# Taking the combination stage out of a graph, mixture-of-experts and LSTM kernel: expert blocks write the final rows

## The reference, cut to what matters

```
x1 = x + L0_gnn(norm(x))                      # first gather over the edges
h  = norm(x1)
idx = argmax(softmax(h @ gate_w)); pos = rank of the token within its expert
kept = pos < 977                               # tokens beyond the capacity get y = 0
y  = expert[idx](h) * (prob * kept)            # two matrix products with a relu between
x2 = x1 + nan_to_num(y)
h2 = norm(x2) @ W
out = segment_sum(dinv[src] * dinv[dst] * h2[src], dst)   # edges, and a self loop for each node
x3 = x2 + leaky_relu(out + b)
```

## Time and profile before

| what | us |
|---|---|
| median of 3 runs (4526.97 to 4539.17) | 4530.03 |
| span of the profiled execution, first to last instruction | 4155.8 |
| experts, 1838 to 2306 | 468 |
| combination, 2306 to 2396 | 90 |
| second gather stage, 2396 to 3426 | 1030 |

### The profile page before, as it was taken

How to read it: one execution, slowest core, us unless ns; L and a number is a source line. 1 busy time by engine, 2 the same in 40 slices (tenths; PEclk the granted TensorE clock), 3 DMA queues, 4 the chain that set the end, 5 groups by cost and what they waited for, 6 DMA issues and landing times. The chain is left out here.

```text
span 4155.8 us, 60925 instructions
## 1 busy us (share of the span) xinstructions
PE 3533.2 (85%) x19537; PEld 2737.7 (66%) x19537; DVE 1869.1 (45%) x5749; ACT 900.6 (22%) x2377; POOL 1671.7 (40%) x1752
## 2 busy tenths in 40 slices
PE   7999999878888888879999455667777779999996
PEld 3444444477777787856666245555555559999996
DVE  4555400133454555643333722233344554444787
ACT  2333333100000011112222500000000004444553
POOL 1000000277777777730110577777777750000000
PEclk9999999887878888869999577787889999999998
DMA  4343444433444444441221643444455555434333
GB/s 149 151 153 150 148 169 168 143 111 113 119 121 131 132 136 139 142 121 43 84 85 54 195 133 106 119 133 133 141 153 159 165 163 163 148 114 121 108 108 114
DMA packets 224399, 544.30 MB, mean 131 GB/s; under 512 B 44131, under 2 KB 125286, under 8 KB 210255
## 3 DMA queue, kind: packets, MB, share of 16 engines
q1 hardware_dynamic: 139744, 314.86, 22.4%
q0 software_dynamic: 80576, 220.31, 18.8%
q10 hardware_dynamic: 3760, 5.24, 0.4%
HBM read 363.08 MB, written 176.74 MB: 130 GB/s over the span
## 5 line engine op out<-in xcount | busy, mean ns | idle before, releaser
L1677 POOL DMA_INDIRECT b_msg<-scratch_gtab,k_src_row x782 | 767.3, 981 | 253.5 <-issue 248.3
L914 POOL DMA_INDIRECT a_msg<-scratch_hrel,k_rel_row x782 | 762.3, 975 | 241.1 <-issue 236.2
L1726 PE MATMUL b_ps<-b_hit,b_msg 128*128 128x128 f32 x3128 | 493.1, 323 | 278.0 <-DMA b_msg<-scratch_gtab,k_src_row 266.4
L706 PE MATMUL r_psm<-k_w,r_xnT 128*128 128x512 f32 x1568 | 693.1, 597 | 5.1 <-ACT r_hst L670 4.2
L1726 PEld LDWEIGHTS b_ps<-b_hit,b_msg 128*128 128x128 f32 x3128 | 460.7, 233 | 350.4 <-issue 270.7
L980 PE MATMUL a_ps<-a_hit,a_msg 128*128 128x128 f32 x3128 | 520.1, 335 | 115.5 <-DMA a_msg<-scratch_hrel,k_rel_row 112.6
L980 PEld LDWEIGHTS a_ps<-a_hit,a_msg 128*128 128x128 f32 x3128 | 479.8, 242 | 146.2 <-DVE a_hit L1102 69.1
L2105 PE MATMUL l_psg<-k_hall,k_whhT 128*128 128x125 f32 x4640 | 550.7, 277 | 5.2 <-DVE k_hall L2231 5.2
L2105 PEld LDWEIGHTS l_psg<-k_hall,k_whhT 128*128 128x128 f32 x4640 | 538.4, 193 | 5.7 <-DVE k_hall L2231 5.7
L706 PEld LDWEIGHTS r_psm<-k_w,r_xnT 128*128 128x128 f32 x1568 | 293.1, 191 | 348.5 <-issue 340.4
L670 ACT COPY r_hst<-r_psm 128x512 f32<-128x512 f32 x392 | 229.2, 586 | 471.6 <-PE r_psm L706 471.6
(11 more groups left out here) (273 smaller groups left out, 3622.4 us busy)
## 6 DMA issues: line engine op xcount, KB each, us to landing
scratch_hrel<-r_hst SPq DMA_DIRECT2D x98, 1024.0 KB
l_xr<-scratch_xrow SPq DMA_DIRECT2D x146, 512.0 KB, 3.6
scratch_xrow<-n_xs SPq DMA_DIRECT2D x50, 512.0 KB, 3.2
a_msg<-scratch_hrel,k_rel_row POOLq DMA_INDIRECT x782, 2.8
b_msg<-scratch_gtab,k_src_row POOLq DMA_INDIRECT x782, 2.8
scratch_ybuf<-x_ys SPq DMA_DIRECT2D x7, 1024.0 KB, 13.7
scratch_xtab<-g_xn SPq DMA_DIRECT2D x49, 132.0 KB, 3.5
scratch_x<-n_xo SPq DMA_DIRECT2D x50, 128.0 KB
```

The costliest lines, as they stand in the source:

```text
L706: mm = pe.matmul(psm[:, c % 4], xnT[:, u, kk], k.w[:, kk, c * 512:(c + 1) * 512], start=(kk == 0), stop=(kk == 1))
L914: pool.indirect_dma_start(msg[:, q, j], None, table, bass.IndirectOffsetOnAxis(ap=rows_of[:, g, j:j + 1].bitcast(U32), axis=0)).then_inc(s ...
L1677: pool.indirect_dma_start(msg[:, q, j], None, k.gtab, bass.IndirectOffsetOnAxis(ap=k.src_row[:, g, j:j + 1].bitcast(U32), axis=0)).then_in ...
L1726: mm = pe.matmul(ps[:, u, kk, 0:WIN], msg[:, g % SL, j, kk * P:(kk + 1) * P], hit[:, u, j], start=(j == 0), stop=(j == pieces(g)[-1]))
```

## The change

`stage_combine` goes, and with it the stores to `ybuf`, `x2` and `gtab` and the gathers of `ybuf`. One table `gx` takes their place; its row holds norm(x2) * dinv (256 floats) and x2 (256 floats), and behind the 49 tiles it has a place for the rows of empty slots.

- First stage: every tile writes default rows, with x1 in place of x2, to `gx` (ACT's `spread` and two stores), and x1 behind the norm in `xtab`, whose row grows from 264 to 520 floats. `slot_read` is no longer computed; `slot_write` (the row of `gx` for each expert slot) is made at the end.
- Expert stage: for each block DVE adds x1, takes the statistics and scales (`rows`, `scale`), ACT takes the root and normalises (`root`, `norm`), POOL scatters 128 rows of 2 KB into `gx` and then fetches the block 16 further on. POOL also clears `k_accT`.
- Second stage: gathers read the first half of the rows of `gx` (index 2 * src). A tile's own row is loaded with x2 (256 KB), turned by PE (`turn_own`) and added to `k_accT` by DVE (`own`) before the tile is finished; SP's stores and loads are ordered by group.

The core of the diff:

```diff
@@ stage_first
+    def spread(t):
+        act.wait_ge(S["xn"], t + 1)
+        if t >= XR:
+            act.wait_ge(s_d[t % XR], 48 * (t // XR))
+        act.activation(gd[:, t % XR], xn[:, t % XN, 0:D], ACT.Copy, scale=k.dinv[:, t:t + 1]).then_inc(S["gd"], 1)
...
+                        for t in begun(g - 3):
+                            sp.wait_ge(S["a"], t + 1)
+                            sp.dma_start(halves(k.xtab[1 + t * P:1 + (t + 1) * P, k.DB:k.XW]), x1(t)).then_inc(s_d[t % XR], 16)
+                            sp.dma_start(halves(k.gx[t * P:(t + 1) * P, D:2 * D]), x1(t)).then_inc(s_d[t % XR], 16)
+                            sp.wait_ge(S["gd"], t + 1)
+                            sp.dma_start(k.gx[t * P:(t + 1) * P, 0:D], gd[:, t % XR]).then_inc(s_d[t % XR], 16)
@@ stage_experts, ACT
+                        if e and i == 2:
+                            root(TB * e - 1)
+                            norm(TB * e - 2)
+                        if e and i == 5:
+                            norm(TB * e - 1)
...
                         act.activation(yg[:, n % 2], y[:, n % 2], ACT.Copy, scale=xr[:, e % 2, n, D:D + 1]).then_inc(S["yg"], 1)
+                        if n >= 1:
+                            root(t - 1)
+                        if n >= 2:
+                            norm(t - 2)
@@ stage_experts, DVE
+                def rows(t):
+                    e, n, u = t // TB, t % TB, t % 2
+                    v.wait_ge(S["yc"], t + 1)
+                    if t >= XO:
+                        v.wait_ge(s_o[t % XO], 16 * (t // XO))
+                    v.tensor_tensor(xo[:, t % XO, D:2 * D], ys[:], xr[:, e % 2, n, k.DB:k.XW], ALU.add).then_inc(S["xa"], 1)
...
@@ stage_experts, POOL
-                for e in range(2, EX):
-                    hold(k, pool, S["yg"], TB * (e - 1))
-                    fetch(e)
+                pool.memset(k.accT[:], 0.0).then_inc(S["az"], 1)
+                for t in range(BL):
+                    hold(k, pool, S["xn"], t + 1)
+                    pool.indirect_dma_start(
+                        k.gx, bass.IndirectOffsetOnAxis(ap=k.slot_write[:, t:t + 1].bitcast(U32), axis=0),
+                        xo[:, t % XO], None).then_inc(s_o[t % XO], 16)
+                    if t + 2 * TB < BL:
+                        fetch(t + 2 * TB)
@@
-def stage_combine(k):
...
@@ stage_second
+                    def turn_own(t):
+                        pe.wait_ge(s_x[t % XB], 16 * (t // XB + 1))
+                        if t >= 1:
+                            pe.wait_ge(S["own"], t)
+                        for kk in range(2):
+                            mm = pe.transpose(pst[:, 1, kk * P:(kk + 1) * P],
+                                              xb[:, t % XB, kk * P:(kk + 1) * P], k.ident[:])
+                        mm.then_inc(S["gt"], 1)
...
+                    def own(t, g):
+                        v.wait_ge(S["gt"], t + 1)
+                        if along:
+                            v.wait_ge(s_add, g)
+                        v.tensor_tensor(k.accT[:, :, t * P:(t + 1) * P], k.accT[:, :, t * P:(t + 1) * P],
+                                        halves(pst[:, 1, 0:2 * P]), ALU.add).then_inc(S["own"], 1)
```

More of the change, by code:

```diff
@@ L1085, in _ @@
                             root(t)
+                        for t in begun(g - 2):
+                            spread(t)
                 @block.vector
@@ L1254, in _ @@
                     v.tensor_copy(k.slot_token[:], listed[:]).then_inc(S["tok"], 1)
+                    done = Chain(v, S["wr"])
+                    v.wait_ge(S["tr"], 2)
+                    done(v.scalar_tensor_tensor(out=blank[:], in0=listed[:], scalar=0.0, in1=trash[:],
+                                                op0=ALU.is_equal, op1=ALU.mult))
+                    done(v.scalar_tensor_tensor(out=k.slot_write[:], in0=listed[:], scalar=-1.0, in1=blank[:],
+                                                op0=ALU.add, op1=ALU.add))
                     v.wait_ge(S["tok"], 8)
@@ L1268, in stage_experts @@
     s_g = [[k.pool_dma_sem(f"x_g{u}{n}") for n in range(TB)] for u in range(2)]
+    s_o = [k.pool_dma_sem(f"x_o{u}") for u in range(XO)]
     halves = [(a, min(a + 512, k.CAP)) for a in range(0, k.CAP, 512)]
@@ L1295, in _ @@
                 sp.dma_start(b1r[:], b1.rearrange("e (f p) -> (e f) p", p=P)).then_inc(S["b"], 16)
[L1296 to L1304, removed]
-                    sp.dma_start(k.ybuf[at:at + P], ys[:, n]).then_inc(S["sc"], 16)
-                sp.wait_ge(S["sc"], 16 * (EX - 1 + TB))
+                for e in range(2, EX):
+                    sp.wait_ge(S["yg"], TB * (e - 1))
+                    weights(sp, e)
             @block.tensor
@@ L1356, in _, with root, norm @@
             def _(act):
+                def root(t):
+                    act.wait_ge(S["var"], t + 1)
+                    act.activation(rstd[:, t % 2, 0:1], mv[:, t % 2, 1:2], ACT.Sqrt, bias=k.eps[:, 0:1]).then_inc(S["std"], 1)
+                def norm(t):
+                    act.wait_ge(S["nm"], t + 1)
+                    act.activation(xo[:, t % XO, 0:D], xo[:, t % XO, D:2 * D], ACT.Identity, bias=rstd[:, t % 2, 3:4],
+                                   scale=rstd[:, t % 2, 2:3]).then_inc(S["xn"], 1)
                 weights(act, 0)
@@ L1556 @@
+                for u in range(XO):
+                    pool.wait_ge(s_o[u], 16 * len(range(u, BL, XO)))
+                pool.wait_ge(S["az"], 1)
 ORDER = (0, 2, 4, 6, 1, 3, 5, 7)
@@ L1563, in stage_second @@
     name = "b_"
-    SL, XR = 7, 4
+    SL, XR, XB = 7, 4, 6
     B = 2 * SL
@@ L1668, in tiles @@
             begun = lambda g: [t for t in range(NT) if first[t] == g]
+            ahead = lambda g, n: [t for t in range(NT) if max(first[t] - n, 0) == g]
             with nc.Block(no_gpsimd_drain=True) as block:
@@ L1769, in _ @@
                             sums(g)
+                        for t in ahead(g, 2):
+                            turn_own(t)
                         for t in begun(g - 4):
@@ L1814, in add @@
                             v.wait_ge(s_add, g)
+                        owned = sum(1 for t in range(NT) if max(first[t] - 1, 0) <= g)
+                        if owned:
+                            v.wait_ge(S["own"], owned)
                         v.tensor_tensor(k.accT[:, :, bass.ds(at, WIN)], k.accT[:, :, bass.ds(at, WIN)],
                                         ps[:, g % 2, :, 0:WIN], ALU.add).then_inc(s_add, 1)
+                    def own(t, g):
[4 more added lines that the diff above has]
+                                        halves(pst[:, 1, 0:2 * P]), ALU.add).then_inc(S["own"], 1)
                     def rows(t):
@@ L1863, in _ @@
                             build(g + 1)
+                        for t in ahead(g, 1):
+                            own(t, g)
                         for t in begun(g - 5):
```

276 lines of the change are left out of this document (103 added, 173 removed).

## The result

| | median, us | ratio to before, 95% interval |
|---|---|---|
| changed kernel | 4471.11 (4462.34 to 4474.76) | 0.9863 [0.9845, 0.9881] |
| before, same runs | 4531.75 | |
| changed kernel, timed again | 4469.74 (4463.15 to 4474.65) | 0.9864 [0.9846, 0.9883] |
| before, same runs | 4527.92 | |

The change takes away 60.6 and 58.2 us. The prediction said 59 us and 4471.

A forecast was written before the change was run, and what follows sets the result against it. POOL's gathers were taken to bound both gather stages, PE the experts, with the combination serial. Removing 93.0 us and paying 20 + 6 + 4 + 1.5 + 2.5 gives -59 us: 4471, range 4448 to 4510.

The forecast's parts named there:

- The stage removed: Combination, from PE's last expert block to the second stage's first gather: all 93.0 us go, except for a new tail.
- The 374 us: Difference between median run 4530.0 and profiled span 4155.8 us, placed around the span and taken as unchanged.
- The tail: After PE's last expert block, up to the second stage's first gather: 20 us of new serial time, bounds 17 and 26.
- the 2.3 us: Part of the tail: 1.0 for the last scatter queued on POOL, 1.3 for longer rows and POOL's issue.
- DVE against PE: Expert blocks: DVE's 4.10 us against PE's 3.67, paid at seven turns to the next expert: 6 us, 0 to 20.
- The start of the experts: Before the first hidden layer, longer rows on full queues delay the weights: 4 us, between 0 and 8.
- The gather stages: Added work mostly hidden behind POOL's gathers: 1.5 us in the first (0 to 6), 2.5 in the second (0 to 21).
- The sum: Whole kernel: -93.0 + 20 + 6 + 4 + 1.5 + 2.5 = -59 us, time 4471.
- (a): Rival, PE never notices: turns 0, start 0, tail 17, gather stages 1.5; -74 us, 4456; chance 0.15.
- (b): Rival, POOL's gathers slow down: 21 us in the second gather stage, 6 in the first; -36 us, 4494; chance 0.14.
- (c): Rival, expert blocks: the scatter's landing paces the loop with three x_xo buffers; 4521 to 4555 us; chance 0.16.
- signs of being wrong: DVE waiting for the scatter, PE waiting inside blocks, first hidden layer over 8 us late, or POOL waiting in gather stages.

The follow-up runs named there:

- e10: The kernel before, no edit, profiled a third time: span 4539.8 us.
- e1: The kernel before, no edit, profiled once more: span 4553.5 us.
- e7: Same kernel as e3, profiled again and timed: median 4454.22 us, ratio to before 0.9832.
- e3: Changed kernel with ACT's root and normalisation at an expert's turn moved behind the third relu, later pairs to the sixth and ninth: span 4473.2 us.
- e2: The changed kernel, no edit, profiled once more: span 4496.5 us.
- e5: Changed kernel plus, per tile, four more DVE additions in the second gather stage and six more 128 KB stores in the first: span 4478.7 us.
- e4: Changed kernel with two buffers instead of three for the scattered rows x_xo: span 4585.5 us.

## Why the prediction was right, step by step

Its time is right, and its tail and its turns are right to about 1 us. The stage removed was larger than it took, the start of the experts cost less, and its picture of the gather stages is wrong. That the total still came out is in part luck.

**The stage removed: 93.0 predicted, 101.4 in usual executions** (101.3 in e10; in e1 from the last bias addition at 2529.52 to 2631.1). The term was read rightly, but from the quick execution. The 374 us that the prediction put around the span are 2 in every other profile; as they stood on both sides, the difference was not touched.

**The tail: 20 predicted, 20.4.** PE, the last bias addition, the last two normalisations, the last scatter and the first gather of the changed kernel, timeline:

```profile
2494.75 24.12 PE L1367 MATMUL x_psy<-x_w2s,x_hT 128*128 128x256 f32 x111
...
2520.43 0.41 DVE L1474 TENSOR_TENSOR x_y<-x_psy,x_b2s 128x256 f32<-128x256 f32 x1
...
2527.45 1.31 ACT L1381 ACTIVATE x_xo<-x_xo,x_rstd 128x256 f32<-128x256 f32 x2
...
2530.41 0.97 POOL L1506 DMA_INDIRECT scratch_gx<-x_xo,k_slot_write  x1 [0.30 <-issue]
2539.30 0.99 POOL L1642 DMA_INDIRECT b_msg<-scratch_gx,k_src_row  x1 [7.93 <-issue]
```

PE ends at 2518.87. DVE starts the last block 1.56 us later (predicted 1.6), the normalisation ends 9.9 us after PE (9.8), and the first gather comes 10.5 us after that (10.2). Of the 2.3 us that were added here by estimate, no row of the prediction shows the parts; the sum of 10.5 bears them out, not each of them.

**DVE against PE: 6 predicted, 7.2.** The iteration is 4.07 us (4.10 predicted, with 0.15 for the add's wait for the copy, where 0.45 less 0.34 is 0.11), in the first expert of the changed kernel:

```profile
2121.90 0.41 DVE L1474 TENSOR_TENSOR x_y<-x_psy,x_b2s 128x256 f32<-128x256 f32 x1
...
2125.97 0.40 DVE L1474 TENSOR_TENSOR x_y<-x_psy,x_b2s 128x256 f32<-128x256 f32 x1
...
2134.24 0.42 DVE L1443 TENSOR_TENSOR x_xo<-x_ys,x_xr 128x256 f32<-128x256 f32 x1 [2.30 <-DMA scratch_gx<-x_xo,k_slot_write]
```

A turn costs 1.0 us on average, not 0.8: from the first gated block of an expert to that of the next it is 55.6 us before and in e7, and 56.4 to 56.8 in the changed kernel, but 57.3 at the last turn. PE's wait is 5.1 us in all, 0.56 to 0.84 at six turns and 1.4 at the last. The pair ahead of the first relu is the root of the seventh and the normalisation of the sixth of the eight blocks, as told; e3 shows that it makes the relu late: with the pair moved (and the two operations behind it later too) the wait is gone.

**The start of the experts: 4 predicted, under 1.** From the first fetch to the hidden layer it takes 18.6 us (2047.61 to 2066.21), where the profile of the prediction has 18.5 (1838.76 to 1857.29) and e1 18.1 (2066.16 to 2084.25). The queues moved more in the same time, 363 instead of 325 GB/s, and carried the rest beside the hidden layer:

```profile
2049.00:2065.00 16.00, 4.89 (x15) 2.10 (x16) 2.97 (x7) 0.00 (x0) 12.25 (x13) 0.50 0.99 363
2065.00:2075.00 10.00, 9.70 (x19) 4.33 (x20) 0.42 (x1) 2.27 (x4) 9.48 (x3) 0.74 0.73 251
```

The step took the rate of full queues as fixed. Its lower bound was the right end.

**The gather stages: 1.5 and 2.5 predicted.** Means of the usual executions: first stage 1264.5 before, 1263.9 in the five with the change; second 1200.5 and 1204.6. That is -0.6 and +4.1, inside the scatter, but from executions on different chips. e1 and e2 ran on one chip, and there the stages are 7.1 and 6.8 us longer with the change. The reason given was wrong: POOL does not set the pace there in a usual execution. That what the change adds is hidden is shown for no more than the adds and stores of e5.

**The sum.** Experts and boundary gain 72.8 us (564.7 to 491.9), where the prediction's terms gave 63. The timed runs show 58 to 61, with an interval of 53 to 70. As the rest of the span repeats, the 12 to 15 us between must lie in the two gather stages, if the timed runs are like the profiled ones; the pair e1 and e2 has 13.9 there, the means above 3.5. The prediction had 4 for them. So two errors of about 10 us, one in the experts and the boundary and one in the gather stages, stand against each other in the total. What makes the gather stages longer is not known. The 2 KB rows of `gx` under the gathers, the loads of 256 KB, PE's turns and ACT's copies are new there too, and no run takes them away.

**The rivals.** (a) fell: PE notices, by 7.2 us. (b) fell: a gather takes 985 ns against 981, and if its stages are 12 to 15 us longer, it is not by slower gathers. (c) fell at three buffers and holds at two. Its formula left out 0.8 us between the normalisation and POOL's scatter, so 5.4 us are free, not 6.2; the landing is 2.85, not 4. Two of the signs of being wrong did come, without their price. POOL waits in the gather stages, but it does so in the usual executions of before too. And the last add of an expert waits 2.1 to 2.4 us for a scatter in six of the eight experts, while the next weights load; in e7 it still does, 13.0 us in all, and no product of the hidden layer waits for ACT. For a 256 KB transfer through POOL's queue the fit of the Trainium skill (DMA: Bandwidth & Descriptors, Anatomy of one DMA — SWDGE (gpsimd) path) gives an estimate of 2.6 us; 2.85 was measured. By the Trainium skill's rule on contention (GPSIMD Engine Reference, section 1, Specifications) a DVE add with one input in PSUM does not hold up POOL; e5's 987 ns agree.

## What to carry to other kernels

Compare the span of a profile with the time of the timed runs before building on it: here 8% between them meant that the profiled execution was not like the timed ones, not that time lies outside the span. A serial stage that only finishes rows can be folded into a loop that another engine bounds, even if the finishing engine becomes a little slower than the loop (4.07 against 3.67 us), as long as a part without its work follows to catch up in: at 5.60 us (e4) it no longer did, and PE waited up to 10.8 us at a turn. Look then at the turn between the two parts, where in-order waits on a third engine hand the delay back: moving these behind independent work gave another 7 us. And a total that comes out is no proof of its terms: compare them one by one.

## What the runs showed of the hardware

In the longer gather stages, and for some 12 us of the combination, instructions that follow each other at once elsewhere start 0.7 to 1.4 us apart on several engines. Weight loads of PE in the changed kernel's first gather stage, then three small DVE operations of the combination in e10, twice, 10 us apart:

```profile
912.60 0.29 PEld L992 LDWEIGHTS a_ps<-a_hit,a_msg 128*128 128x128 f32 x1 [0.41 <-issue]
913.30 0.28 PEld L992 LDWEIGHTS a_ps<-a_hit,a_msg 128*128 128x128 f32 x1 [0.41 <-issue]
...
2535.22 0.13 DVE L1532 RECIPROCAL c_rstd<-c_rstd 128x1 f32<-128x1 f32 x1
2535.39 0.16 DVE L1534 TENSOR_TENSOR c_rstd<-c_rstd,k_dinv 128x1 f32<-128x1 f32 x1
2535.58 0.16 DVE L1536 SCALAR_TENSOR_TENSOR c_rstd<-c_mv,c_rstd 128x1 f32<-128x1 f32 x1
...
2545.76 0.14 DVE L1532 RECIPROCAL c_rstd<-c_rstd 128x1 f32<-128x1 f32 x1
2546.66 0.16 DVE L1534 TENSOR_TENSOR c_rstd<-c_rstd,k_dinv 128x1 f32<-128x1 f32 x1 [0.75 <-DVE c_rstd L1532]
2547.36 0.16 DVE L1536 SCALAR_TENSOR_TENSOR c_rstd<-c_mv,c_rstd 128x1 f32<-128x1 f32 x1 [0.54 <-issue]
```

The distance from the first to the third of the DVE operations is 0.36 us and then 1.60. Three iterations take 12.0 us there (2540.35 to 2552.37 from add to add) instead of 3 x 1.50, which is 7.5 of the 8.3 us by which the boundary is longer. The expert stage repeats to 0.3 us. The stretches fall where POOL issues gathers back to back, in every profile but that of the prediction; fewer sums and fewer bytes leave most of the time in place, so the link with the gathers is seen, not shown. A scatter of 256 KB to memory lands 2.85 us after its start in e4's blocks, where no weights load, and 6.5 us (2127.70 to 2134.24 in the changed kernel) while they do.
